# Moving group loads and stores from SyncE's queue to ScalarE's, and spreading out transposes, in a fused attention and expert layer

## The reference

```python
xn = layernorm(x)
# attention, causal, with a bias that grows with the key's position
scores = einsum('bqe,bke->bqk', xn @ W_qk, xn) / 16 + (kpos - qpos) * slope
s = softmax(where(causal, scores, -inf)) @ (xn @ W_v.T)
# 8 experts, each takes at most 512 of the 4096 tokens, in order of tokens
probs = softmax(xn @ Wr); e = argmax(probs); p = probs[e]
rank = how many earlier tokens chose e; keep = rank < 512
y[token] = keep * p * (relu(xn @ W1[e]) @ W2[e])
out = x + s * silu(y)
```

## Time and profile before

| | us |
|---|---|
| median of 3 runs | 438.6 (438.42 to 440.61) |
| the profiled execution, its own time | 441.75 |
| its span, first to last instruction | 440.0 |
| granted TensorE clock over the span | 1.000 |
| TensorE busy | 420.4 (96%) |
| VectorE busy | 322.4 (73%) |
| ScalarE busy | 222.7 (51%) |
| GpSimd busy | 228.3 (52%) |

### The profile page before, as it was taken

How to read it: one execution, slowest core, us unless ns; L and a number is a source line. 1 busy time by engine, 2 the same in 40 slices (tenths; PEclk the granted TensorE clock), 3 DMA queues, 4 the chain that set the end, 5 groups by cost and what they waited for, 6 DMA issues and landing times.

```text
span 440.0 us, 8367 instructions
## 1 busy us (share of the span) xinstructions
PE 420.4 (96%) x3015; PEld 288.6 (66%) x3015; DVE 322.4 (73%) x838; ACT 222.7 (51%) x444; POOL 228.3 (52%) x353
## 2 busy tenths in 40 slices
PE   6899999998999899999989999999999999999996
PEld 2667576756668676766666666666666666665666
DVE  5989778988888478778747787979796967424553
ACT  3755454452657146545424555545455545454551
POOL 3257851826544826056102566575757576757530
PEclk9999999999999999999999999999999999999999
DMA  7996898366945634266866577676888873234840
GB/s 238 294 294 151 277 295 191 74 130 163 279 90 111 139 115 117 57 216 153 120 96 232 165 245 226 205 250 176 281 156 280 179 206 98 90 120 113 159 98 31
DMA packets 104280, 76.01 MB, mean 173 GB/s; under 512 B 73263, under 2 KB 98108, under 8 KB 102192
## 3 DMA queue, kind: packets, MB, share of 16 engines
q1 hardware_dynamic: 92976, 53.11, 47.3%
q0 software_dynamic: 5824, 16.74, 12.9%
q10 hardware_dynamic: 5440, 5.64, 3.9%
HBM read 31.33 MB, written 28.58 MB: 136 GB/s over the span
## 4 chain that ended last, share of the span: by engine, by line
PE 64%; DVE 13%; DMA 11%; issue 4%; ACT 4%; POOL 1%; SPq 1%; another core or an unknown queue 0%; ACTq 0%; POOLq 0%; DVEq 0%
PE bank L1419 18%; PE bank L1421 18%; PE bank L1420 17%; DMA xg<-in_x 4%; DMA pT<-p_rows 3%; PE bank L1510 3%; DVE sc L1012 3%; PE bank L1513 3%; PE bank L1512 3%; PE bank L1491 2%; ACT sc L1269 2%; DVE p_rows L1033 2%; DMA rows<-xg 1%; DMA slots<-xnr,slot_idx 1%; DMA xeT<-slots 1%
## 5 line engine op out<-in xcount | busy, mean ns | idle before, releaser
L1510 PE MATMUL bank<-v_h,pT 128*128 128x257 f16 x272 | 74.7, 274 | 3.2 <-DMA pT<-p_rows 3.2
L1513 PE MATMUL bank<-v_h,pT 128*128 128x257 f16 x272 | 74.1, 272 | 0.0
L1512 PE MATMUL bank<-v_l,pT 128*128 128x256 f16 x272 | 73.7, 271 | 0.0
L1296 ACT ACTIVATE hid_h<-bank 128x512 f16<-128x512 f32 x64 | 38.1, 596 | 67.7 <-PE bank L1421 59.8
L1102 DVE SCALAR_TENSOR_TENSOR hid_l<-bank,hid_h 128x512 f16<-128x512 f32 x64 | 44.0, 688 | 38.0 <-ACT hid_h L1296 33.7
L1421 PE MATMUL bank<-w_h,hid_l 128*128 128x256 f16 x256 | 69.8, 273 | 0.0
L1419 PE MATMUL bank<-w_h,hid_h 128*128 128x256 f16 x256 | 69.8, 273 | 0.0
L1420 PE MATMUL bank<-w_l,hid_h 128*128 128x256 f16 x256 | 69.8, 273 | 0.0
L1012 DVE CUSTOM_DVE_ANT_0 sc<-bank,bias,score_mul 128x512 f32<-128x512 f32 (+2 forms) x80 | 52.9, 664 | 9.1 <-PE bank L1421 9.0
L1419 PE MATMUL bank<-xT,qT_h 128*128 128x512 f16 (+3 forms) x160 | 55.0, 347 | 3.1 <-DVE cmin L1012 1.7
L1285 ACT ACTIVATE pT<-bank 128x512 f16<-128x512 f32 (+3 forms) x50 | 24.6, 494 | 60.3 <-PE bank L1491 50.9
(11 more groups left out here) (198 smaller groups left out, 919.9 us busy)
## 6 DMA issues: line engine op xcount, KB each, us to landing
raw<-in_w_e SPq DMA_DIRECT2D x5, 2048.0 KB
sc<-in_w_e SPq DMA_DIRECT2D x3, 2048.0 KB
slots<-empty ACTq DMA_DIRECT2D x1, 4224.0 KB, 18.7
gates<-gate SPq DMA_DIRECT2D x8, 512.0 KB
out<-xg SPq DMA_DIRECT2D x7, 512.0 KB
rows<-xg SPq DMA_DIRECT2D x7, 512.0 KB, 7.2
rows<-so SPq DMA_DIRECT2D x7, 512.0 KB
xg<-in_x SPq DMA_DIRECT2D x6, 512.0 KB, 4.4
```

What stands on the lines that cost most here:

```text
L1296: a_.activation(hid_h[:, f % HB, :], sc_ps[f % 2][:, :], ACT.Relu).then_inc(h_hi, 1)
L1510: pe.matmul(pv_ps[t % 2][:, 0:D + 1], p_h, v_h[:, at, q, 0:D + 1], start=kb == 0, stop=False)
L1512: pe.matmul(pv_ps[t % 2][:, 0:D], p_h, v_l[:, at, q, :], start=False, stop=False)
L1513: last = pe.matmul(pv_ps[t % 2][:, 0:D + 1], p_l, v_h[:, at, q, 0:D + 1], start=False, stop=kb == t % NT)
```

## The change

Three things. `group_out`, `group_in` and `group_s` are written once more on ScalarE, and for `group_out(2)` to `(6)`, `group_in(2)` to `(5)` and `group_s(0)` to `(5)` ScalarE issues the DMAs, as well as the first two loads of weights, at the end of the steps that three tables name. SyncE keeps groups 0 and 1. `turn(g)` becomes `turn(g, j)`, one transpose, and those of groups 4 to 7 are issued one at a time after the chunk of a step: group 4 in tile 11, group 5 in tile 15, group 6 in tile 16, group 7 in tiles 21 and 22. And the last group's units move: VAL and VAL + 1 to (23, 0), VAL + 2 and VAL + 3 to (23, 1), RANK from (25, 0) to the last step of tile 24.

```diff
             end = {REST - 8: [SPLIT] * first,
-                   REST - 5: [VAL, VAL + 1] * last,
-                   REST - 4: [VAL + 2, VAL + 3] * first + [PICK] * (c == 1),
-                   REST - 3: [RANK] * first,
+                   REST - 5: [VAL, VAL + 1] * first + [VAL + 2, VAL + 3] * (c == 1),
+                   REST - 4: [PICK] * (c == 1) + [RANK] * last,
                    REST - 2: [QRY, QRY + 1] * last}.get(t, [])
...
+        def turns_after(t, c):
+
+            if t in (3, 6):
+                return [(t // 3 + 1, j) for j in range(GT) if last_step(t, c)]
+            if t == 11:
+                return [(4, j) for j in range(GT) if min(j, 2) == c]
+            if t in (NT - 1, NT):
+                return [(t - 10, c)]
+            if t in (REST - 7, REST - 6) and c < 2:
+                return [(LATE, (t - REST + 7) * 2 + c)]
+            return []
...
-        SECOND_LOAD = 23
+        FIRST_LOAD, SECOND_LOAD = (6, 0), (23, 1)
+        OUT_AT = {(4, 0): 2, (8, 0): 3, (10, 0): 4, (12, 0): 5, (17, 0): 6}
+        IN_AT = {(5, 1): 2, (9, 0): 3, (11, 1): 4, (13, 2): 5}
+        S_AT = {(6, 1): 0, (9, 2): 1, (13, 0): 2, (18, 0): 3, (21, 1): 4, (25, 1): 5}
...
+            group_out(1)
             for t in range(REST):
-                g = t // GT
-                if t % GT == 0 and g + 1 < LATE and g + 1 != NG + 1:
-                    group_out(g + 1)
-                if t % GT == 1:
-                    if g + 1 <= NG:
-                        group_in(g + 1)
-                    if g:
-                        group_s(g - 1)
                 if t == 1:
+                    group_in(1)
                     rows_of(1)
-                if t == 5:
-                    sp.dma_start(raw[:, :, :], w_k[0]).then_inc(w_in[1], 16)
-                if t == SPLIT_TILE[NG + 1]:
-                    group_out(NG + 1)
                 for c in steps(t):
                     if by_dma(t, c):
                         chunk_turn(t, c)
-                if t == SPLIT_TILE[NG + 1]:
-                    group_in(NG + 1)
-                for n in (*SPLIT_TILE, LATE):
-                    if t == {5: 14, LATE: REST - 8}.get(n, SPLIT_TILE.get(n)):
-                        turn(n)
+                    for g, j in turns_after(t, c):
+                        turn(g, j)
                 if t == FIRST_SCALE - 1:
                     spread(0)
-                if t == SECOND_LOAD:
-
-                    sp.wait_ge(w_lo, 2 * PIECES)
-                    sp.dma_start(raw[:, :, :], w_k[1]).then_inc(w_in[1], 16)
...
+            def transfers(t, c):
+                if (t, c) in OUT_AT:
+                    group_out(OUT_AT[t, c])
+                if (t, c) in IN_AT:
+                    group_in(IN_AT[t, c])
+                if (t, c) in S_AT:
+                    group_s(S_AT[t, c])
+                if (t, c) == FIRST_LOAD:
+                    act.dma_start(raw[:, :, :], w_k[0]).then_inc(w_in[1], 16)
+                if (t, c) == SECOND_LOAD:
+
+                    act.wait_ge(w_lo, 2 * PIECES)
+                    act.dma_start(raw[:, :, :], w_k[1]).then_inc(w_in[1], 16)
...
                     for g, n in units_after(t, c):
                         if n == PICK:
                             chance(g)
+                    transfers(t, c)
```

More of the change, by code:

```diff
@@ L499, in spread, with turn @@
                 sp.dma_start(wall[:, :], tops[e, 0:2 * P].partition_broadcast(P)).then_inc(w_spread, 16)
-            def turn(g):
+            def turn(g, j):
                 at = key_slot(g // NG, g % NG)
@@ L506, in turn @@
                     sp.wait_ge(score_full, chunk_no(NT, 0))
-                for j in range(GT):
-                    sp.wait_ge(xn_lo, rows_to(g))
-                    sp.dma_start_transpose(xT[:, at, j, :, :], halves[g % NX][:, j, :]).then_inc(xT_in[g % NX], 16)
+                sp.wait_ge(xn_lo, rows_to(g))
+                sp.dma_start_transpose(xT[:, at, j, :, :], halves[g % NX][:, j, :]).then_inc(xT_in[g % NX], 16)
             def rows_of(g):
@@ L1353, in _, with group_out, group_in, group_s @@
                 unit(0, n)
+            def group_out(g):
+                k, n = g % 2, (g // 2 + 1) * 16
+                act.wait_ge(x_in[k], n)
+                act.dma_start(out_g[g], xg[k][:, :, :]).then_inc(out_first[k], 16)
+                act.dma_start(rows_g[g][:, :, 0:D], xg[k][:, :, :]).then_inc(rows_x[k], 16)
+            def group_in(g):
+                k, n = g % 2, (g // 2 + 1) * 16
+                act.wait_ge(xn_made, made_to(g))
+                act.wait_ge(out_first[k], n)
+                act.wait_ge(rows_x[k], n)
+                act.dma_start(xg[k][:, :, :], x_g[g + 2]).then_inc(x_in[k], 16)
+            def group_s(g):
+                act.wait_ge(s_made, g * GT + GT)
+                act.dma_start(rows_g[g][:, :, D:2 * D], so[g % 2][:, :, :]).then_inc(rows_s[g % 2], 16)
+            def transfers(t, c):
[10 more added lines that the diff above has]
+                    act.dma_start(raw[:, :, :], w_k[1]).then_inc(w_in[1], 16)
             def tile(t):
```

## The result

The changed kernel takes **443.6 us** (median, 443.18 to 444.58), the kernel before 438.5 in the same comparison: ratio 1.0113, 95% interval 1.0080 to 1.0145. In a second comparison it was 1.0108 (1.0080 to 1.0136). It is slower by 1.1%, or 5 us, and above the range that was forecast (434.4 to 441.2). Executions more than 1.5% above the fastest of the same kernel in a comparison are left out of every ratio.

What follows compares the result with a forecast made beforehand. TensorE was taken to bound the kernel (busy 52.0 of 55 us in 80:135), so only its idle time could be won. 0 - 0.65 + 0.3 = -0.35 on the 438.6 median gave 438.2; own range 437.0 to 440.2, overall 434.4 to 441.2.

Steps and rivals of the forecast that it cites:

- the slower rival: At the scale in (12, 2): group 5's stores delay the spread to 112.0, 4.4 us late; 441.4 us, chance 0.14.
- part 2: Loads and stores issued by ScalarE: 22 issues, about 12 us on ScalarE, 0 in the sum, 0 to 1 in range.
- part 1: Group 4's turns between chunks of tile 11: 1.82 us won at (11, 0), given back at the scale; 0.
- a recovery: From the scale in (12, 2) to (15, 1): VectorE's idle time takes back 1.5 to 1.6 of 1.8 us lateness.
- part 4: Last two groups' units: new 1.7 us stall at group 6's ranking, +0.47 at group 7's; +0.3 (-0.6 to +1.45).
- the wait meant to swallow it: First expert's tokens, set by GpSimd: TensorE wants them at 220.5, they come at 222.56; stall of 1 to 2 us stays.
- 1.84 us at the tokens: TensorE's stall at 221.11 for the first expert's tokens, one of five stalls summing to 6.43 us.
- 0.64 at 131.14: TensorE's stall where a score waits until VectorE has read an earlier one; 0.64 us, forecast to stay.
- Two of the waits meant for it: VectorE's waits for x at 115.62 and 128.88, 0.21 and 0.61 us, to go as ScalarE loads x earlier.
- its threshold of 109.2: Landing time of the spread for the scale in (12, 2), after which the slower rival decides.
- my own bound, 109.4: Latest landing of the spread for the scale in (12, 2), 1.8 us after the 107.64 of before.
- Part 3: Turns of groups 5 to 7: the 1.35 us stall at (15, 1) loses 1.24 or nothing; half taken, -0.65.

Runs made afterwards that it cites:

- the two usual ones: The kernel before, without an edit, run again: the two profiled executions of 438.81 and 438.32 us, near its median.
- the turns alone: Kernel before with only the transposes of groups 4 to 7 issued one at a time between chunks, all transfers by SyncE: ratio 1.0016.
- turns and moves: Changed kernel with the last groups' units back where they were, keeping single transposes and ScalarE's loads and stores: 1.0097; loads and stores alone, in before: 1.0001.
- the last repair: Four of ScalarE's transfers moved away from SyncE's transposes, in the changed kernel with maximum a tile earlier and units back: 1.0004, from 1.0045.
- the late spread: Kernel before with the spread of the first weights' maximum sent behind the two stores at the start of tile 12: ratio 1.0074.
- the three repairs: Changed kernel with the maximum one tile earlier, the last groups' units back, and four of ScalarE's transfers away from SyncE's transposes: ratio 1.0004.
- Apart: Changed kernel with four of ScalarE's transfers moved to other steps, away from SyncE's transposes: ratio 1.0086.
- the stores late: Changed kernel with the two stores of group 5 at the end of (12, 3) and not of (12, 0): ratio 1.0084.
- the tops first: Changed kernel with group 4's last transpose moved between the write of the tops and the spread: ratio 1.0109.
- turns with the early maximum: Kernel before with transposes of groups 4 to 7 one at a time and the first maximum a tile earlier, transfers by SyncE: 0.9995 and 1.0035.
- the experiment above: Changed kernel with the maximum of the first weights one tile earlier and the last groups' units back where they were: ratio 1.0045.

## Why the prediction was wrong

The forecast was 438.2 with a range up to 441.2; the slower rival said 441.4, outside that range. 443.6 was measured. Two terms of the sum failed in their mechanism: part 2, put at 0, left out what ScalarE's transfers do to SyncE's beside them, and part 1 counted on a recovery that didn't come. In part 4 TensorE's own loss was right, and the wait meant to swallow it wasn't there.

**The starting point.** I priced 1.84 us at the tokens and 0.64 at 131.14 as if every execution had them. Neither is in the two usual ones. The profile's own time, 3.2 us above the median, was the sign: I put the difference on the median, but not on the stalls.

**Part 1** forecast 0: 1.82 won, all given back at the scale. The chain up to VectorE came as written: tops at 101.65 (measured 101.6 with the turns alone), spread at 104.85 (104.8), read by 109.4 (109.1). What failed is the recovery: "1.5 to 1.6 of 1.8" should have come back by (15, 1). Two of the waits meant for it were waits for x, which can't go while SyncE loads it (VectorE still waits 0.86 us for x at 116.61 in the kernel with the turns alone, and not in the changed one); of 1.84 us at the scale (109.11 for 107.27) 0.7 came back, and turns alone cost 1.14 us on TensorE's path and 0.7 by the timing. In the changed kernel the slower rival is what happened: the stores of group 5 under the tops, a read at 110.54, beyond its threshold of 109.2. I gave it 0.14 though my own bound, 109.4, already lay past that threshold. It had the place and the mechanism right but the wrong transfer: its 7.2 us were for the spread, while it was the tops that were held (5.5, and 7.2 in the second profile), and its 2.8 us of lateness were 1.66 at (13, 0).

**Part 2** forecast 0, and by the timings this is the step that carries most of the error: turns and moves cost 4.3 us together, 0.7 and 0 alone. How much of that is this mechanism isn't shown: taking the transfers away from the transposes gave back 1.0 us in the changed kernel and 1.8 as the last repair. I priced what the 22 issues cost ScalarE, and the landing of ScalarE's own transfers, but not what those do to SyncE's transposes beside them. The 3.26 us from issue to landing at (11, 0) was read in a stretch where no such transfer ran; in the new order the load of group 6 starts 0.5 us behind it, and it took 5.4, in other kernels 6.5. The Trainium skill ("DMA: Bandwidth & Descriptors", Issuing engines are not separate DMA queues) says that DMAs of all engines run on the same 16 DMA engines and interleave. I took from it only that no transfer gets faster. It gives no price for what interleaving does to the transfers of others; here four transposes that took 5.80 us took 6.37, 7.08 and 8.36 beside ScalarE's stores. What the issues cost ScalarE, some 12 us in all and in the sum 0, wasn't harmless either: one of 1.77 us started the loss of 2.9 us in the profiled execution with the units back.

**Part 3** forecast -0.65 at (15, 1), if the four transposes issued before it held it. They didn't: the wait is 1.34 to 1.90 in all kernels of this study, whatever stood ahead in the queue. In the usual execution of before it took 4.7 us to land, and the four transposes behind it 6.02 where four others took 5.13:

```profile
91.23 5.13 SPq L509 DMA_TRANSPOSE xT<-xnr  x4
...
141.63 6.02 SPq L509 DMA_TRANSPOSE xT<-xnr  x4
```

The DMA view of 140 to 146 in that execution (queue, kind: packets, MB, share of 16 engines over the stretch) has one packet of 16 KB of instructions in it, for 1.2% of 96 us, or 1.15 us on one of the 16 engines:

```profile
q1 hardware_dynamic: 2146, 0.52, 77.9%
q8 instruction: 1, 0.02, 1.2%
```

In every trace of this study such a packet starts 1.2 to 2.4 us behind the issue of (15, 1), wherever that lies (142.15 here, 144.14 with the late spread), and the transpose takes 4.5 to 5.0 us where its landing is recorded. That it holds the transpose is argued from this and wasn't tried.

**Part 4** forecast +0.3, with TensorE's own stalls at 1.7 and +0.47, and +1.24 in all at the tokens. These came: 1.57 and 0.45, TensorE 1.38 to 1.54 later. The step that failed is the last: I let GpSimd and the tokens decide, so that most of it would vanish in a wait that was there anyway. In a usual execution it isn't, and by the traces the whole 1.4 to 1.5 counts (by the timings 0.6 and 0.9, and 1.5 as a repair).

**The clock** was in no case of mine. After holes of 1.9 and 2.55 us the clock fell to its lower level for part of the next 8 us and cost some 1.7 us in the profiled execution. In a third profile it fell after a hole of 2.03 us near 46. That this joins the parts (turns make TensorE early, the late spread and the slow transposes make it wait, and a long hole can bring the clock down) is argued: the holes behind which it fell lie at three different places, and most executions of the changed kernel kept the full clock.

In the sum, by the trace of the changed kernel: 1.66 at the scale for part 1's and part 2's 0; 1.95 at (15, 1) for part 3's -0.65, of which 0.3 is the longer wait and 1.65 the clock; 1.53 at the units for part 4's +0.3. Together 5.1 for -0.35. Other executions lose about as much in other places, so the total is firmer than its parts.

**What stays open.** In executions of the changed kernel at full clock the time is still 442.3 to 445.2, 3 us and more over before; the three repairs take away the whole only together. Apart, late and the stores late are some 1.5 us slower by the timing than by their traces, the tops first 2.4 us (its profiled execution was the shortest of its six). And whether turns with the early maximum pay isn't settled by two comparisons.

## What to carry to other kernels

Before you move transfers to another engine's queue, list which transfers that the critical engine waits for will then be under way at the same time, and price those at the landing times of a stretch with such traffic, not at those of a quiet one. Follow a gain to the next thing that is sent through the same queue (here a maximum, two DMAs and 8 us away from its reader): making it a tile earlier took the wait away here, and shortening its way by one step only moved it. Count also what each issue holds the engine that now makes it, at its longest and not only in the median. When the profiled execution lies above the median, take no stall of it for granted before a second one shows it.

## What the runs showed of the hardware

- A DMA transpose of a chunk landed 3.3 us after its issue with no bulk transfer beside it, 5.4 and about 6.5 with one load of half a megabyte issued half a us later by another engine, and again within 3.3 with the load issued 2.9 us earlier. A small write (the tops) took 3.0 to 3.7 us with no store or load beside it, 5.5 to 7.2 just behind two stores of another engine, and 5.0 behind two of its own. The spread scattered from 3.0 to 6.1 us, with and without stores beside it.
- Issuing the second of two stores of half a megabyte held ScalarE for 0.5 to 1.5 us, and once for 1.77.
- One packet of instructions, 16 KB, kept a DMA engine for 0.9 to 2.8 us. It starts 1.2 to 2.4 us behind the issue of (15, 1) in every trace.
- The granted clock fell after idle stretches of TensorE of 1.9 us (to a mean of 0.69 over 4 us, then 0.89), 2.55 us (0.84, 0.73) and 2.03 us (0.57), but not after the 1.8 to 1.9 us at (11, 0) in before, nor after the 2.35 us at 50.51 in the experiment above (1.00). What else it takes, no run here tells.
- The same program scatters by 1.4 to 6 us from execution to execution, and its traces differ too: the four of before start (25, 0) within 1.4 us of each other. A stall of 1 us can be placed in a trace, and hardly be told by 12 timed executions.
